# A four-layer graph network on one core: small block products in place of block-diagonal ones, and a bias by TensorE

## The reference

```
h = max(layernorm(x), 0);  x = x + L0(h, adj)   # attention, 8 heads of 32, biases in q, k, v and out;
                                                # heads 0-5 have fixed masks, 6 and 7 have adj | eye
h = max(layernorm(x), 0);  x = x + L1(h, adj)   # attention, 4 heads of 64, every head masked by adj
h = max(layernorm(x), 0);  x = x + L2(h, adj)   # gated graph attention, 4 heads of 256:
     Wh = h W + bW;  e = Wh attn;  A = tanh(where(adj, e Wh^T, 0));  hp = relu(A Wh)
     ha = cat(hp) A_w^T;  hf = h fc_w^T;  c = sigmoid(hf g1^T + ha g2^T + b);  out = hf c + ha (1 - c)
h = max(layernorm(x), 0);  x = x + L3(h, adj)   # 8 heads of 32: cosine links times softmax weights,
     sem = h gmap^T + bias;  out = relu((links * p) sem gcn_W^T / (sum + 1))
```

## Time and profile before

| | us |
|---|---|
| median of three runs (2073.71 to 2076.98) | 2075.4 |
| the profiled execution, its own time | 2077.8 |
| its span | 2075.8 |
| TensorE busy, records | 1953.7 (94%), 22672 |
| VectorE busy | 1450.1 (70%) |
| ScalarE busy | 897.8 (43%) |
| GpSimd busy | 600.1 (29%) |

### The profile page before, as it was taken

How to read it: one execution, slowest core, us unless ns; L and a number is a source line. 1 busy time by engine, 2 the same in 40 slices (tenths; PEclk the granted TensorE clock), 3 DMA queues, 4 the chain that set the end, 5 groups by cost and what they waited for, 6 DMA issues and landing times. The chain is left out here.

```text
span 2075.8 us, 61017 instructions
## 1 busy us (share of the span) xinstructions
PE 1953.7 (94%) x22672; PEld 1834.2 (88%) x22672; DVE 1450.1 (70%) x3183; ACT 897.8 (43%) x1866; POOL 600.1 (29%) x685
## 2 busy tenths in 40 slices
PE   7999999799999889999999999999999798888887
PEld 7888888799999789999999999999999788888886
DVE  6889998577777545555555555555555389999998
ACT  6777777555555422222322232232222244444443
POOL 4555555322222011111011111111111154544443
PEclk9999999999999999999999999999999899999998
DMA  3222222343232201110011110011111012222221
GB/s 100 77 77 62 77 70 69 113 122 93 77 93 81 81 22 32 32 32 21 26 31 31 31 31 29 18 31 31 31 31 31 26 43 61 63 61 62 66 62 58
DMA packets 149378, 113.43 MB, mean 55 GB/s; under 512 B 42945, under 2 KB 148801, under 8 KB 149313
## 3 DMA queue, kind: packets, MB, share of 16 engines
q1 hardware_dynamic: 149312, 112.52, 18.8%
HBM read 78.93 MB, written 33.55 MB: 54 GB/s over the span
## 5 line engine op out<-in xcount | busy, mean ns | idle before, releaser
L275 POOL TENSOR_TENSOR ln_rstd<-ln_var_eps,minus_half 128x2 f32<-128x2 f32 x128 | 90.8, 709 | 798.1 <-DVE ln_var_eps L268 796.9
L1705 ACT ACTIVATE l_cat_hi<-banks 128x512 fp32r<-128x512 f32 x128 | 76.5, 598 | 260.1 <-PE banks L1876 260.1
L182 PE MATMUL banks<-ln_hT_hi,square_w_hi_held 128*128 128x256 f32 x512 | 151.7, 296 | 3.2 <-DVE square_w_lo_held L658 3.2
L292 ACT ACTIVATE ln_h<-ln_x,ln_shift,ln_rstd 128x256 f32<-128x256 f32 x256 | 139.7, 597 | 31.2 <-DVE ln_shift L282 26.7
L182 PE MATMUL banks<-ln_hT_hi,l_g_w_hi 128*128 128x256 f32 x512 | 148.8, 291 | 4.1 <-PEq L1974 4.1
L182 PE MATMUL banks<-l_cat_hi,l_aw_hi 128*128 128x256 f32 x512 | 144.5, 282 | 0.0
L183 PE MATMUL banks<-ln_hT_lo,square_w_hi_held 128*128 128x256 f32 x512 | 143.0, 279 | 0.0
L184 PE MATMUL banks<-ln_hT_hi,square_w_lo_held 128*128 128x256 f32 x512 | 142.6, 279 | 0.0
L184 PE MATMUL banks<-ln_hT_hi,l_g_w_lo 128*128 128x256 f32 x512 | 142.5, 278 | 0.0
L183 PE MATMUL banks<-ln_hT_lo,l_g_w_hi 128*128 128x256 f32 x512 | 142.5, 278 | 0.0
L183 PE MATMUL banks<-l_cat_lo,l_aw_hi 128*128 128x256 f32 x512 | 141.7, 277 | 0.0
(11 more groups left out here) (238 smaller groups left out, 6678.2 us busy)
## 6 DMA issues: line engine op xcount, KB each, us to landing
hidden<-y SPq DMA_DIRECT2D x96, 256.0 KB, 2.1
ln_x<-hidden SPq DMA_DIRECT2D x96, 256.0 KB, 2.8
x_res<-hidden SPq DMA_DIRECT2D x96, 256.0 KB, 3.0
ln_x<-x SPq DMA_DIRECT2D x32, 256.0 KB, 2.9
x_res<-x SPq DMA_DIRECT2D x32, 256.0 KB, 3.1
out<-y SPq DMA_DIRECT2D x32, 256.0 KB, 2.2
l_adj_u<-adj SPq DMA_DIRECT2D x96, 16.0 KB, 2.4
l_stage_attnT<-L_attnT SPq DMA_DIRECT2D x4, 256.0 KB, 3.6
```

Of the source, the lines that this page charges most:

```text
L182: nc.tensor.matmul(out, lhs(lh), rhs(rh), start=start, stop=False, skip_group_check=True)
L275: self.nc.gpsimd.tensor_tensor(self.rstd[:, g.slot], self.var_eps[:, g.slot], self.core.minus_half[:, 0:PAIRS], ALU.pow).then_inc(self.rst ...
L292: last = self.nc.scalar.activation(self.h[:, u, p, :], self.x[:, u, p, :], ACT.Relu, bias=self.shift[:, u, p:p + 1], scale=self.rstd[:, u, ...
L1705: nc.scalar.activation(cat_hi[:, h * KC:(h + 1) * KC], halves(B_HP[h]), ACT.Relu).then_inc(cat_hi_ready.sem, 1)
```

## The change

Four parts, by layer.

1. Layers 0 and 1: `k_bd` and `v_bd` go, with their memsets. K and the values are copied as they are (K whole, by ScalarE alone), and scores and weighted values are formed by products of one head and one board: 32 (layer 0) or 64 rows for the scores, 64 rows (the tokens of one board) for the values. For this each head of a chunk has a bank of its own, four (2 to 5) in layer 0 and two in layer 1, and the rows of softmax are in another order. In layer 0 K^T moves to bank 0, beside hT, the output product shares bank 3 with the scores, and so has to wait for them to be read; ScalarE's order becomes q, exponential 0, k, exponential 1; VectorE forms hT_lo of the group before between the two parts of the statistics; LayerNorm's transposes stand between the two transposes of weights.
2. Layer 2: `a_bd` becomes `a`, GpSimd fills heads 0 and 1, VectorE 2 and 3. hp is made of 64x64 blocks, of two heads at a time. Wh goes in six units, 512, 512, 256, 260, 256 and 260 columns, the two of 512 between the two halves of the head products. ha is in two banks and is rounded in halves.
3. Layer 3: the bias of the last dense product is added by a product with rows of ones and the bias's high and low part (512 columns). The values' copies are ScalarE's for one board of a pair and VectorE's for the other. y is formed by GpSimd, the relu moves into the product with `factor`. ScalarE's order becomes exponential 0, nT, q, k, exponential 1.
4. SyncE issues ln.load a step earlier in all layers.

The core of the diff (waits and index arithmetic that only follow are left out):

```diff
@@ SyncE, all four layers
-                gn = ln.group(g)
+                gn = ln.group(g.back(-1))
-            run_steps(sp, step, groups, 3)
+            run_steps(sp, step, groups, 3, ahead=2)
@@ attention_layer
-        k_bd = sb("k_bd", [P, 2, KC, NB, HPC, S], F32, MOVED)
-        v_bd = sb("v_bd", [P, 2, PAIRS, 2, HH, 2, VW], F32, HELD if direct else MOVED)
+        k = sb("k", [P, 2, KC, TOK], F32, MOVED)
+        v = sb("v", [P, 2, PAIRS, 2, HPC, VW], F32, HELD if direct else MOVED)
-        B_Q, B_K, B_V, B_PROJ = 1, 2, 1, 3
-        B_S, B_O = 4, 6
+        B_Q, B_K, B_V, B_PROJ = 1, 0 if direct else 2, 1, 3
+        B_S, B_O = 2 if direct else 4, 6
@@ attention_layer, scalar
+                    for c in range(KC):
+                        last = nc.scalar.activation(v[c * S:(c + 1) * S, b1.slot, :, 0, :, 0:HD], heads_of_v(0, c), ACT.Copy)
...
+                    evacuate_T(q, B_Q, 0).then_inc(q_ready.sem, 1)
+                if direct and c2.exists(groups):
+                    exponential(0)
+                if b1.exists(groups):
+                    after(act, k_in_psum, b1)
+                    evacuate_T(k, B_K, 1).then_inc(k_ready.sem, 1)
+                if direct and c2.exists(groups):
                     exponential(1)
@@ attention_layer, vector
                 if direct:
+                    prev = ln.group(g.back(1))
                     if gn is not None:
                         ln.statistics(dve, gn, first=True)
+                    if prev is not None:
+                        after(dve, v_in_psum, prev.back(2))
+                        ln.evacuate_lo(dve, prev, B_HT)
+                    if gn is not None:
                         ln.statistics(dve, gn, first=False)
...
-                            if bk is not None:
-                                last = nc.vector.tensor_scalar(dst[:, c], src[:, c], b_col[r0:r0 + HD, 1, c:c + 1], None, ALU.add)
@@ attention_layer, tensor: scores
-                                    last = nc.tensor.matmul(
-                                        ps[b * S:(b + 1) * S, B_S + t, col:col + HPC * S],
-                                        q[:, u, c, pb * S:(pb + 1) * S], k_bd[:, u, c, pb],
-                                        start=False, stop=True, skip_group_check=True)
+                                for hp in range(HPC):
+                                    r = slice(hp * HD, (hp + 1) * HD)
+                                    last = nc.tensor.matmul(ps[b * S:(b + 1) * S, B_S + hp, col:col + S],
+                                                            q[r, u, c, toks], k[r, u, c, toks],
+                                                            start=False, stop=True, skip_group_check=True)
@@ attention_layer, tensor: values (layer 1, then layer 0)
+                                        last = nc.tensor.matmul(
+                                            ps[b * S:(b + 1) * S, B_O + c, col:col + VW],
+                                            probT[r, u, 0, hp * PAIRS + p, b * S:(b + 1) * S],
+                                            v[r, u, p, b, hp], start=True, stop=True, skip_group_check=True)
...
+                                            last = nc.tensor.matmul(
+                                                ps[hp * HD:(hp + 1) * HD, B_OT + c, col:col + S], v[r, u, p, b, hp],
+                                                probT[r, u, t, (hp - 2 * t) * PAIRS + p, b * S:(b + 1) * S],
+                                                start=True, stop=True, skip_group_check=True)
@@ attention_layer, tensor: output product, transposes
+                    if direct:
+                        after(pe, shifted_ready, c2, 1)
...
-                    for t in range(NT):
-                        transpose_prob(weighted, weighted_ready, t)
+                    transpose_prob(weighted, weighted_ready, 0)
...
                     ln.transpose(pe, gn, B_HT)
+                if direct and c2.exists(groups):
+                    transpose_prob(weighted, weighted_ready, 1)
@@ graph_attention_layer
-    THIRDS = ((0, 320), (320, 384), (704, WC - 704))
+    UNITS = ((0, 0, 512), (1, 0, 512), (0, 512, 256), (0, 768, WC - 768), (1, 512, 256), (1, 768, WC - 768))
-        a_bd = sb("a_bd", [P, PAIRS, H, 2, S], F32, MOVED)
+        a = sb("a", [P, PAIRS, H, S], F32, MOVED)
+                    for hh in range(2):
+                        h = 2 * k + hh
+                        for c in range(KC):
+                            for p in range(PAIRS):
+                                col = ((hh * KC + c) * PAIRS + p) * S
+                                for half in range(2):
+                                    f0 = h * D + c * P + half * S
+                                    for b in range(2):
+                                        r = slice(b * S, (b + 1) * S)
+                                        last[b] = nc.tensor.matmul(ps[half * S:(half + 1) * S, B_HP[b], col:col + S],
+                                                                   wh[r, p, f0:f0 + S], a[r, p, h], start=True, stop=True)
...
+                    for c in range(KC):
+                        after(act, ha_in_psum, c2, c + 1)
+                        nc.scalar.activation(ha_hi[:, c], ha(c), ACT.Copy).then_inc(ha_hi_ready.sem, 1)
@@ gated_graph_layer
+                if e.exists(groups):
+                    after(pool, t_ready, e)
+                    after_dma(pool, x_res_loaded, e)
+                    after_dma(pool, y_stored, e.back(2))
+                    nc.gpsimd.tensor_tensor(y[:, e.slot], t[:, e.slot], x_res[:, e.slot], ALU.add).then_inc(y_ready.sem, 1)
...
+                        last = nc.scalar.activation(v[c * S:(c + 1) * S, b1.slot, :, 0, :, 0:HD], heads_of_sem(0, c), ACT.Copy)
...
+                        last = nc.vector.tensor_copy(v[c * S:(c + 1) * S, u, :, 1, :, 0:HD], heads_of_sem(1, c))
...
+                if bias is not None:
+                    nc.tensor.matmul(ps[:, bank, :], two_ones[:], bias_rows[:, bias].unsqueeze(1).to_broadcast([P, PAIRS, D]),
+                                     start=True, stop=False, skip_group_check=True)
...
-                    exponentials(1)
                 if b1.exists(groups):
...
                     with_bias(k, B_K, 1).then_inc(k_ready.sem, 1)
+                if c2.exists(groups):
+                    exponentials(1)
```

More of the change, by code:

```diff
@@ L108, in after_dma, with run_steps @@
             eng.sem_inc(apart.waits_passed.sem, 1)
-def run_steps(eng, step, groups, lag):
+def run_steps(eng, step, groups, lag, ahead=0):
     head = (lag + 3) // 2 * 2
-    body = (groups - head) // 2 * 2
+    body = (groups - head - ahead) // 2 * 2
     for s in range(head):
@@ L643, in step @@
                                              ACT.Copy).then_inc(probT_ready.sem, 1)
-                if not direct and b1.exists(groups):
-                    evacuate_v()
                 if gn is not None:
@@ L777, in _ @@
         def _(pe):
[L778 removed]
+            pe.wait_ge(core.constants_ready.sem, 1)
             if first:
@@ L1172, in step @@
             def step(g):
-                gn = ln.group(g)
-                if g.reg is None and g.c == EarlyLoads.FIRST:
+                gn = ln.group(g.back(-1))
+                if g.reg is None and g.c == EarlyLoads.FIRST - 1:
                     after_dma(sp, y_stored, Group(None, -2))
@@ L1278, in step @@
                     with_bias(k, B_K, 1).then_inc(k_ready.sem, 1)
+                if c2.exists(groups):
+                    exponentials(1)
                 if gn is not None:
                     ln.apply(act, gn)
+                if b1.exists(groups):
+                    if b1.reg is None and b1.c == 0:
+                        act.wait_ge(preset.sem, 1)
+                    after(act, sem_in_psum, b1)
+                    after(act, o_in_psum, b1.back(2))
+                    for c in range(KC):
+                        last = nc.scalar.activation(v[c * S:(c + 1) * S, b1.slot, :, 0, :, 0:HD], heads_of_sem(0, c), ACT.Copy)
+                    last.then_inc(sem_act_ready.sem, 1)
                 if c2.exists(groups):
@@ L1501, in step @@
                     after(pe, sem_ready, b1.back(1))
+                    after(pe, sem_act_ready, b1.back(1))
                     project(2, b1, B_M).then_inc(m_in_psum.sem, 1)
@@ L1775, in step @@
                     after(dve, yT_in_psum, e.back(1))
-                    nc.vector.scalar_tensor_tensor(out=yT[:], in0=part[:], scalar=0.5, in1=halves(B_HA), op0=ALU.mult,
-                                                   op1=ALU.add).then_inc(blend_steps.sem, 1)
+                    for c in range(KC):
+                        last = nc.vector.scalar_tensor_tensor(out=yT[:, c], in0=part[:, c], scalar=0.5, in1=ha(c), op0=ALU.mult,
+                                                              op1=ALU.add)
+                    last.then_inc(blend_steps.sem, 1)
                 if gn is not None:
@@ L1823, in step @@
                 if c2.exists(groups):
```

(5 more changed lines are left out.)

472 lines of the change are left out of this document (234 added, 238 removed).

## The result

The changed kernel takes 1967.03 us (median of 4 runs, 1964.95 to 1967.4), beside 2076.19 for the kernel before (4 runs, 2073.71 to 2076.99) on the same chip. The ratio of the two is 0.9474, 95% interval 0.9458 to 0.949: 109 us faster. The forecast was 1941, its range 1905 to 1990.

A forecast was written before the change was run, and what follows sets the result against it. TensorE was taken to bound layers 1 and 2, VectorE layer 3, both near in layer 0. Gains of 43.5, 24, 41 and 26 us (layers 0 to 3) sum to 134.5, taking 2075.4 to 1941 us, range 1905 to 1990.

The forecast's parts named there:

- The gate's wait: Layer 2: the gate product's wait for ha_lo shrinks as ha is rounded by halves; 0.2 us a group.
- The last step: Layer 2: 24 products taking 2.7 us cover the 2.2 us until two banks are read, 0.5 to spare.
- The 0.13 for Wh's columns: Layer 2: Wh's 1028 columns as 256, 256, 256 and 260 save about 0.13 us a group.
- own work forecast 9.77: Layer 0: TensorE's work without waits falls from 10.48 to 9.77 us a group; with 0.1 for meetings, 9.9.
- hT_lo is formed ahead of it, which moves it out of that overlap: Layer 0, VectorE: ln_var_eps (1.17 us) no longer runs beside GpSimd's subtraction; counted as 0.9 us a group.
- 0.71 for products: Layer 0, TensorE: values, scores and masks as small blocks take 2.56 instead of 3.27 us a group.
- 0.65 for waits: Layer 0: TensorE's 0.78 us wait a group for the weighted probabilities goes; 0.1 is added for meetings.
- the loop binds: Layer 3: the loop scores, softmax, link, transposes, LayerNorm's transposes, masks binds both engines, about 11.6 us; 11.75 taken.
- D: Rival: edits work as said, but blocks of 64 rows add up to 22 ns; 1964 us, chance 0.17.
- A: Rival: blocks as priced, but layer 0 keeps its 0.78 wait and layer 3 stays at 12.2; 1980 us, chance 0.17.
- B: Rival: blocks of 64 rows are as fast as those of 32, 14 ns; 1898 us, chance 0.13.
- C: Rival: blocks don't overlap, all 320 new records a group run one after another at 29.7 ns; 2081 us, chance 0.03.

The follow-up runs named there:

- lo_late: Changed kernel, but in layer 0 VectorE forms hT_lo at the end of its step again, as before: 1965.55 us, ratio 0.9473 to the kernel before.
- only_l2: Changed kernel with layers 0, 1 and 3 taken from the kernel before: 2027.99 us, ratio 0.9753 to the kernel before.
- only_l3: Changed kernel with layers 0, 1 and 2 taken from the kernel before: 2056.72 us, ratio 0.9897 to the kernel before.
- no_bias: Changed kernel without the product adding the bias of layer 3's last dense product, so the result lacks it: 1963.89 us, ratio 0.9455 to the kernel before.
- rows_first: Changed kernel, but layer 2's head blocks of one board all come before those of the other: 2019.65 us, ratio 0.9734 to the kernel before.
- cut_all: cut_attn, and layer 3's TensorE loop body also cut, behind the query product: 1953.56 us, ratio 0.9413 to the kernel before.
- hoist: Changed kernel, but in layers 0 and 1 TensorE's waits for the next scores stand ahead of the values' products: 1966.31 us, ratio 0.9463 to the kernel before.
- cut_attn: Changed kernel with TensorE's loop body in layers 0 and 1 cut behind the key product: 1956.04 us, ratio 0.9418 to the kernel before.
- waits8: Changed kernel plus 8 fulfilled TensorE waits in layers 0 and 1, ahead of masks or between q and k: 1967.67 us, ratio 0.9476 to the kernel before.
- best: cut_all with three of layer 0's masks between the values' halves and layer 3's values behind the first dense product: 1959.44 us, ratio 0.9432 to the kernel before.

## Why the forecast was right, and where it was not

The direction, the range and the mechanism in layers 1 to 3 were right; in layer 0 the forecast had the shares of its two causes wrong. 24 us of 134.5 did not come, and it would be 29 without the 4.5 that layer 2 gave beyond its forecast.

- **Layer 2** (41 forecast, 45.5): 128 records at 17.0 instead of 19.2 ns give 3.40 - 2.18 = 1.22 instead of 0.94 us. The gate's wait went whole, 0.3 instead of 0.2. The last step, that 24 products cover the reading of the banks, held: no idle time stands in front of the second half. The 0.13 for Wh's columns did not come: from start to start its products took 5.79 us a group before and take 5.84 now. (The forecast set 0.16 for 320 columns, with the switch of form, against 0.113 for 256 without it; with it, 256 columns take 0.122.) The steady gain is 1.48, 1.27 forecast.
- **Layer 1** (24, 13.3): the blocks' own price was right (19.4 ns for the values). What the sum lacked is what stands between them. From masks to scores 0.34 instead of 0.21, the jump (0.24 in every second group), scores 0.63 to 0.74 instead of 0.61. That is 1.83 and 1.70 in the two groups, 1.77 instead of 1.44 a group: 0.33 x 32 = 10.6 us, the whole miss.
- **Layer 0** (43.5, 28.7): own work forecast 9.77, steady period 10.21. The rows give: wait for the second transposed weights 0.20, jump 0.13 (0.26 in every second group), rest of the values 0.07, masks 0.13, scores -0.06, the rest -0.03. I had allowed 0.1 for such things. The wait of TensorE for the weighted probabilities is gone, as forecast (0.5 us in 200), and neither of the two order edits that were undone brings it back. Here my step "hT_lo is formed ahead of it, which moves it out of that overlap" is refuted: ln_var_eps is short either way. In the changed kernel and in lo_late VectorE comes to it before GpSimd's subtraction starts (206.35 against 207.68 us, 207.03 against 207.45); which edit brought that about, no run tells.
- **What the collision in layer 0 was worth.** The trace of before has it both ways (the two lines are in the last section). In the six groups whose ln_var_eps takes 0.16 us the period from one subtraction to the next is 10.32 to 10.48 us, and TensorE does not wait for the weighted probabilities; in the other 25 it is 11.19 to 11.88 and TensorE waits. only_l2 and only_l3, with the same old layer 0, show the same. So the collision cost about 1.0 us a group, some 24 us in all, and against a group without it, 10.40, the changed 10.21 is 0.19 shorter. The forecast had seen this collision in one group, but not that it set the period. Most of layer 0's 28.7 us is the collision that went; its small blocks and other edits gave about 0.2 us a group, where the forecast had 0.71 for products and 0.65 for waits.
- **Once in layer 0**, not foreseen: the first pass of the loop, below, some 3 us.
- **Layer 3** (26, 22.9; steady 0.79 a group, 0.82 forecast): the loop binds, as forecast, at 12.13 steady where I had 11.75. I had compared with an average period of 12.57 that holds the faster last groups; the steady one was 12.92. Both periods were read too low by about as much, which is why the gain came out right: in part luck. The bias product's 0.33 instead of 0.23 cost nothing, as no_bias shows.
- **Rivals.** 1967 lies beside D's 1964 by chance, D is wrong: its blocks of 22 ns are 17.0 and 19.4. A took layers 0 and 3 for the place of the loss; layer 1 and its jump were in neither. B's 14 ns appeared for blocks of 32 rows only. C did not come because rows (and banks) alternate, and rows_first shows what it would have been in layer 2.

## What to carry to other kernels

Order small blocks so that neighbours lie on different rows and, as here, in different banks, whatever their columns. Price a run of blocks with what stands at its ends (a change of form, a wait, the jump of a loop), and cut a loop where long products run. An engine that is busy 96% can still be waiting for a loop: take a piece of its work away and look whether the period falls before optimising it. And look at the spread of one instruction's durations and of the groups' periods within one trace: where both jump together, as with ln_var_eps, the trace of before already tells what the collision costs.

## What was not expected of the hardware

**Time between short blocks.** In a pair of groups the jump costs about 0.2 to 0.4 us of TensorE's idle time behind blocks of 14 to 20 ns, and a fulfilled wait 26 ns. Between products of 113 ns the jump cost 0.08 us (cut_all, layer 1), and eight waits showed nothing. That TensorE's instructions are dealt out in turn and run ahead only beside long products fits all of hoist, cut_attn, cut_all, waits8 and best; it was not measured by itself.

**A small VectorE instruction beside GpSimd.** In the kernel before, a group in which ln_var_eps starts just ahead of the subtraction, with the subtraction itself:

```profile
258.02 0.16 DVE L268 SCALAR_TENSOR_TENSOR ln_var_eps<-ln_mean_var 128x2 f32<-128x2 f32 x1
258.03 1.31 POOL L513 TENSOR_TENSOR l_oT_lo<-l_oT,l_oT_hi 128x512 fp32r<-128x512 f32 x1 [2.13 <-ACT l_oT L585]
```

Up to 371 us there are 34 ln_var_eps. The 25 that start while the subtraction runs take 0.55 to 1.28 us, and each ends 13 to 20 ns after the subtraction does; the other nine take 0.16 us, this one included. So this instruction is held until the subtraction is over. VectorE's ln_mean_var, which starts inside the subtraction 20 times, keeps its 0.15 to 0.18 us: not every instruction is held, and why this one is, no run shows.

**The first pass of a loop.** TensorE of the changed kernel, in layer 0:

```profile
49.81 0.85 PE L843 MATMUL banks<-l_k,l_q 32*64 32x64 f32 x57
52.17 0.34 PE L843 MATMUL banks<-l_k,l_q 32*64 32x64 f32 x7 [1.51 <-issue]
...
53.04 0.42 PE L181 MATMUL banks<-ln_hT_hi,l_w_lo_held 128*128 128x256 f32 x1
53.25 0.41 PE L179 MATMUL banks<-ln_hT_hi,l_w_hi_held 128*128 128x256 f32 x1
...
56.08 0.28 PE L181 MATMUL banks<-ln_hT_hi,l_w_lo_held 128*128 128x256 f32 x1
56.20 0.28 PE L179 MATMUL banks<-ln_hT_hi,l_w_hi_held 128*128 128x256 f32 x1
```

TensorE stops 1.51 us in the midst of 64 blocks, and then products of 256 columns start 0.21 us apart, which is the level of 1.2 GHz, until 55.8 us; then 0.11. The window from 52 to 56 us has a granted clock of 0.57. This group took 13.4 us, 3.2 more than the rest. The same stretch in cut_all has a longer stop, 1.83 us, and yet a clock of 1.00, and its group takes 12.1, 2.05 more than the rest. So of the changed kernel's 3.2 an estimated 1.7 are the stop and 1.5 the clock; why the clock fell in one and not in the other is not shown. Kernels with the old layer 0 have no such group; all with the new one have one or two, of 1 to 5 us more. Its cause is open: at this point the loop is entered and TensorE's code is longer (the queue of instruction loads moves 60 packets in the whole, 46 before), and the DMA queues are 82% busy with loads of data from 49 to 52 us. No run tells these two apart.
